# Narrower gram blocks relayed two rows at a time, expert work pulled into the last recurrent step, and constant products on an idle TensorE

## What is computed

```python
def ff_step(W, inp):                                   # fast weights, per head
    v_old = jnp.einsum('bhij,bhj->bhi', W, kt)
    W = W + (bt * (vt - v_old))[..., :, None] * kt[..., None, :]
    z = jnp.einsum('bhij,bhj->bhi', W, qt)
def rec_step(carry, inp):                              # 16 steps, each needs the last one's h
    q_rec = jax.nn.softmax(h, axis=-1)
    v_old = jnp.einsum('bhij,bhj->bhi', R, kt)
    R = R + (bt * (vt - v_old))[..., :, None] * kt[..., None, :]
    h = zt + jnp.einsum('bhij,bhj->bhi', R, q_rec)
...
logits = jnp.mean(x, axis=1) @ Wr + br                 # x: normalised h, 16 x 128 x 64
routing_weights = jax.nn.softmax(logits, axis=-1)
expected_loads = routing_weights.sum(axis=0) * (N / B)
scale = jnp.where(expected_loads > capacity, capacity / expected_loads, 1.0)
routing_weights = jax.nn.softmax(routing_weights * scale, axis=-1)
top_w, top_i = jax.lax.top_k(rw_tok, K); top_w = jax.nn.softmax(top_w, axis=-1)
h = jax.nn.gelu(jnp.einsum('nd,edf->enf', xf, W1) + b1[:, None, :])
y = jnp.einsum('enf,efd->end', h, W2) + b2[:, None, :]  # weighted over the experts, added to x
```

## Times and profile before

| | us |
|---|---|
| three runs | 750.50, 737.28, 741.24; median 741.24 |
| the profiled execution, its own time | 740.56 |
| its span in the trace | 738.7 |
| granted TensorE clock, mean over the span | 0.91 |

### The profile page before, as it was taken

The page is one execution under the profiler, slowest core; times in us unless marked ns, Lnnn a source line. Parts: engine busy times, 40 slices in busy tenths (PEclk is TensorE's granted clock), DMA queues, the critical chain, the costliest instruction groups (busy, mean ns, idle before and its releaser), DMA issues.

```text
span 738.7 us, 12304 instructions
## 1 busy us (share of the span) xinstructions
PE 606.3 (82%) x4657; PEld 477.8 (65%) x4657; DVE 445.8 (60%) x1113; ACT 280.9 (38%) x502; POOL 360.0 (49%) x414
## 2 busy tenths in 40 slices
PE   6889999999987707788877888456999698899996
PEld 3657777785556606677776777352678487785776
DVE  3643444236667756787899999952553736663533
ACT  0075453528966602111110000006553337566550
POOL 1696333218018836797899998143463300001334
PEclk9999999999989956888999999755999869999999
DMA  7000000000004450000000000000000000000000
GB/s 242 1 1 1 2 1 1 0 1 1 0 10 75 78 88 4 1 1 1 1 1 1 1 1 1 0 1 0 1 1 1 1 1 2 1 2 1 8 8 14
DMA packets 10699, 10.35 MB, mean 14 GB/s; under 512 B 5905, under 2 KB 9681, under 8 KB 10385
## 3 DMA queue, kind: packets, MB, share of 16 engines
q1 hardware_dynamic: 7424, 7.12, 3.6%
q0 software_dynamic: 2496, 2.04, 2.0%
q10 hardware_dynamic: 720, 0.41, 0.3%
HBM read 5.70 MB, written 0.52 MB: 8 GB/s over the span
## 4 chain that ended last, share of the span: by engine, by line
PE 55%; DVE 26%; ACT 7%; DMA 4%; issue 4%; POOL 3%; SPq 0%; ACTq 0%; DVEq 0%; POOLq 0%
PE bank L1059 8%; PE bank L1047 7%; DVE features L1743 6%; DVE bank L1777 5%; DVE features L1766 5%; PE bank L1315 4%; PE bank L1136 4%; PE bank L1333 4%; PE bank L1331 4%; PE bank L1403 2%; PE bank L1096 2%; PE bank L1391 2%; PE bank L1127 2%; PE bank L1105 2%; DMA RK<-in_wf 1%
## 5 line engine op out<-in xcount | busy, mean ns | idle before, releaser
L1136 PE MATMUL bank<-ident,features 128*128 128x128 f32 x920 | 126.9, 297 | 63.1 <-DVE features L1743 39.3
L1136 PEld LDWEIGHTS bank<-ident,features 128*128 128x128 f32 x920 | 113.8, 155 | 73.4 <-DVE features L1743 48.0
L506 POOL TENSOR_TENSOR features<-UV,coefs 128x1024 f32<-128x1024 f32 (+1 forms) x64 | 117.6, 1864 | 25.7 <-DVE UV L1730 12.5
L1743 DVE TENSOR_TENSOR features<-UV,bank 128x1024 f32<-128x1024 f32 (+3 forms) x64 | 66.2, 1066 | 0.9
L685 ACT ACTIVATE G<-bank,cols 128x512 f32<-128x512 f32 x64 | 43.3, 687 | 49.5 <-PE bank L1047 49.5
L1047 PE MATMUL bank<-xs,weights 128*128 128x512 f32 x128 | 60.2, 615 | 2.3 <-ACT xs L676 2.3
L1059 PE MATMUL bank<-weights,G 128*128 128x128 f32 x512 | 59.8, 275 | 0.0
L1059 PEld LDWEIGHTS bank<-weights,G 128*128 128x128 f32 x512 | 58.4, 192 | 0.0
L349 POOL TENSOR_SCALAR rstd<-mv 128x4 f32<-128x4 f32 x8 | 1.9, 238 | 112.2 <-DVE mv L361 112.2
L752 ACT ACTIVATE hsT<-bank 128x256 f32<-128x256 f32 x16 | 6.2, 385 | 102.3 <-PE bank L1136 102.3
L1127 PE MATMUL bank<-features 32*128 32x136 f32 x768 | 34.8, 320 | 10.5 <-DVE G L1703 4.1
(11 more groups left out here) (312 smaller groups left out, 1350.6 us busy)
## 6 DMA issues: line engine op xcount, KB each, us to landing
weights<-in_w SPq DMA_DIRECT2D x2, 1024.0 KB, 11.8
features<-in_tok SPq DMA_DIRECT2D x1, 768.0 KB, 6.3
weights<-in_ew SPq DMA_DIRECT2D x4, 128.0 KB, 3.0
weights<-in_ew SPq DMA_DIRECT2D x2, 256.0 KB, 2.9
coefs<-G POOLq DMA_DIRECT2D x20, 25.5 KB, 3.9
coefs<-xs POOLq DMA_DIRECT2D x20, 25.5 KB, 5.2
coefs<-weights POOLq DMA_DIRECT2D x20, 25.5 KB, 5.3
coefs<-sx POOLq DMA_DIRECT2D x18, 25.5 KB, 5.0
```

What stands on the lines that cost most here:

```text
L506: pool.tensor_tensor(out, u, co, ALU.mult).then_inc(s["held_p"], 1)
L1136: last = mm(out[:, P * k:P * k + P], x[:, P * k:P * k + P], ident[:], is_transpose=True, start=first and k == 0, stop=last_ and k == n - 1 ...
L1743: dve.tensor_tensor(out, u, co.unsqueeze(3).broadcast_to([P, R, NH, DH]), ALU.mult)\
```

## The change

Groups of positions become four (GB = 4, NG = 32), and two of them are done together: NR = 16 rounds. A round's products are 48 of 64 x 68, written to the lower and the upper 64 rows of the eight banks. Copies have 204 columns instead of 408. A relay moves 32 rows of 408 to two adjacent partitions, so a round has four relays of 52,224 bytes: two from SP, two from POOL, none from ACT. Six half-size staging buffers lie in G, xs and weights. Sums for steps 4 to 15 move into steps 0 to 4. The statistics and the normalisation of chunk 0 move into steps 5 and 8; its turn, products and GELUs move into step 15, ahead of the rec read-outs. `out_projection` of the last step comes ahead of the means; the three exponentials run without GELUs between them, and chunk 1's GELUs follow. Nine products of `ident` and `rows` follow the grams, one and three more stand around the router's products.

```diff
-GB = 8
+GB = 4
 NG = P // GB
+NR = NG // 2
-NS = 4
+NS = 6
+REWARM = 9
...
-        stage = [b.rearrange("p (b c s) -> p b c s", b=GB, s=SL)
-                 for b in (G[:].rearrange("p g n -> p (g n)")[:, 0:GB * ROWC], XS[:, 0:GB * ROWC], WA[:, 0:GB * ROWC],
-                           SX[:, 0:GB * ROWC])]
+        stage = [b[:, n * GB * ROWC:(n + 1) * GB * ROWC].rearrange("p (b c s) -> p b c s", b=GB, s=SL)
+                 for b in (G[:].rearrange("p g n -> p (g n)"), XS[:], WA[:]) for n in range(2)]
...
         def expert_bank(k, c, e):
+            if k == 0 and c == 0:
+                return bank[4 + e % 2]
...
         def relay(eng, g, j):
-            b = NG * j + g
-            eng.dma_start(CF[b:b + 1, 0:T * ROWC].rearrange("p (t x) -> p t x", t=T),
-                          stage[g % NS][j:P:GB, j].rearrange("p c s -> p (c s)"))\
+            b, x = NG * j + 2 * g, g % NS
+            eng.dma_start(CF[b:b + 2, 0:T * ROWC].rearrange("p (t x) -> p t x", t=T),
+                          stage[x][j:P:GB, j].rearrange("p c s -> p (c s)"))\
...
-                for j in range(0, 3):
+                for j in (0, 1):
                     relay(sp, g, j)
...
-                for j in range(3, 6 if g == NG - 1 else GB):
+                for j in (2, 3):
                     relay(pool, g, j)
...
+                if t == 2 * CH - 1:
+                    rstd_pool(pool, ch, ("f0", 0), CH)
                 held(t)
...
-            for j in (6, 7):
-                relay(act, NG - 1, j)
...
+                if t == T - 1:
+                    experts(0, 0)
+                    expert_gelus(0, 0)
                 state(t)
+            experts(0, 1)
             act.wait_ge(s["mean_mm"], 1)
             act.activation(meanT[:], bank[7][0:D, 0:T], ACT.Copy, scale=1.0 / P).then_inc(s["mean_ready"], 1)
-            experts(0, 0)
             for j in range(3):
                 act.wait_ge(s["r_sub"], j + 1)
                 act.activation(rsel[0:T, j, :], rsel[0:T, j, :], ACT.Exp).then_inc(s["r_exp"], 1)
-                expert_gelus(0, 0, 2 * j, 2 * j + 2)
-            expert_gelus(0, 0, 6, E)
+            expert_gelus(0, 1, 0, 4)
...
                         for j in range(4):
                             x = slice(DH * j, DH * j + DH)
-                            last = mm(bank[4 * k + j][:, GB * SL * n:GB * SL * n + GB * SL],
-                                      feat[left + k][x, g, 0:T].rearrange("p s b -> p (s b)"),
-                                      feat[right + k][x, g].rearrange("p s b -> p (s b)"), start=True, stop=True)
+                            for h in range(2):
+                                last = mm(bank[4 * k + j][D * h:D * h + D, GB * SL * n:GB * SL * n + GB * SL],
+                                          feat[left + k][x, 2 * g + h, 0:T].rearrange("p s b -> p (s b)"),
+                                          feat[right + k][x, 2 * g + h].rearrange("p s b -> p (s b)"), start=True, stop=True)
...
+            def idle_products(b, n):
+                for k in range(n):
+                    mm(b[:, 0:512], ident[:], rows[:, 0:512], start=True, stop=True)
+            pe.wait_ge(s["load_rows"], 48)
+            idle_products(bank[7], REWARM)
...
                 queries(t)
+                if t == T - 1:
+                    pe.wait_ge(s["load_experts"], 16 * 17)
+                    pe.wait_ge(s["pad"], 2)
+                    turn_x(0, 0)
+                    expert_up(0, 0)
                 read_out("rec", t, reads_of("rec", t))
...
+            expert_up(0, 1, 2, 4)
+            pe.wait_ge(s["x_gelu"], E)
+            idle_products(bank[4], 1)
             pe.wait_ge(s["r_prob"], 1)
             mm(bank[7][0:T, 96:96 + E], ones[0:T, 0:T], rout[0:T, 0, :], start=True, stop=True).then_inc(s["load_mm"], 1)
-            expert_up(0, 0, 2, 6)
+            turn_x(0, 2)
+            idle_products(bank[4], 3)
             pe.wait_ge(s["r_spread"], 1)
...
+                if t == CH + 1:
+                    x_stats(0)
+                if t == 2 * CH:
+                    x_apply(0)
+                if t == 0:
+                    normalisers(slice(CH, T))
+                if t == 1:
+                    ch.settle()
+                    strengths(slice(CH, T))
+                if t >= 2 and t + 2 < 2 * CH - 1:
+                    query_scale(t - 1)
                 if t + 1 < T:
                     next_query(t + 1)
```

More of the change, by code:

```diff
@@ L658, in _ @@
         def _(act):
-            ch = Chain(act, s["act_chain"])
             for t, n in ((embT, "embT"), (wupd, "wupd")):
@@ L1786, in read_coefficients, with x_stats @@
                 ch.settle()
+            def x_stats(c):
+                norm_stats(dve, ch, ("f0", c), [H[:, t, :] for t in range(CH * c, CH * c + CH)])
             def x_apply(c):
```

188 lines of the change are left out of this document (94 added, 94 removed).

## The result

The changed kernel takes 766.8 us (median of 4 executions, 765.1 to 772.0) against 739.9 us: a ratio of 1.039, 95% interval 1.033 to 1.045. It is slower by 27 us where 28 us less were forecast. The profiled execution took 765.1 us, with a span of 763.2. From here on every time is the median of those executions of a kernel that lie within 1.5% of its fastest one, which leaves out a few slower ones, such as the 750.5 us of the kernel before.

The account below looks back on a forecast made before the run. Transfers at 70 to 85 GB/s were taken to bound the relays, usually DVE the steps, and a chain of small things the stretch behind. Terms summed to -27.8 from 740.56, giving 712.8 us; own range 706 to 720, 8 in 10 699 to 736.

Parts of the forecast that it names:

- The relays, -8.3: Relay stretch: at 85 GB/s, 3.34 MB take 39.3 us, so the last relay lands at 260.9 instead of 269.18.
- third rival: Relays: writes jam in half as many places, rate halves to 36 to 42 GB/s, 752 to 766 us; chance 0.08.
- The second rival: Relays: few engines serve each two-row transfer, last relay lands at 281.6, +12.4, 733 us; chance 0.18.
- Preparation, -3.0: From last relay to POOL's first product: 3.95 us instead of 7.0, with less scaling ahead of the steps.
- Steps, +4.0: Steps: sums moved into early steps and chunk 0's statistics and normalisation in steps 5 and 8 together add 4.0 us.
- -1.5 for the clock: Start of steps: nine constant products end 2 us ahead of the first step and raise TensorE's clock; bounds -4, +4.
- -0.5 for step 15: Step 15: turn and eight expert products fill an idle hole, state saved at 484.1 instead of 484.6; bounds -1.5, +3.
- To the router's first product, -8.5: From the end of the rec products: reordered projection, statistics and normalisation bring the router's first product at 490.6, 8.5 us less.
- Router, -3.7: Router's first product to weights, 13.4 us before: exponentials no longer wait for GELUs and table changes, 3.7 us less.
- weights to bias, -4.6: From router weights to the bias being added: only the bias work remains, 3.4 us instead of 8.0.
- To the end of the first expert_down, -1.7: From added bias: TensorE stops after two tiles until DVE finishes positional logits; 11.1 us against 12.8.

Follow-up runs that it names:

- the variant without the jam: Changed kernel with the two element groups of a round g and g + 16, so each relay's two destination rows lie 16 apart: 732.5 us, 0.990.

## Why the prediction was wrong

**The relays, -8.3 forecast, +32.1 measured.** The step that failed is the rate: "I take the transfers' own rate, 85 GB/s", because "what set the pace before is still there". It carried the rate of before over to rounds that write to other rows. The text had the right mechanism as its third rival (all bytes of a round to four pairs of neighbouring rows, half as many places, the rate halved to 36 to 42 GB/s, last landing at 300 to 314) and gave it 0.08. The windows read 42 to 45 where all wait (52 at the start), the whole stretch 39, the landing was 301.24, and the variant with rows 16 apart takes the loss back. What was held against that rival, rates over 80 with three neighbouring rounds in flight, was no evidence: in the kernel before, the rows of one round are spread over eight groups of four, and three neighbouring rounds still keep to much the same eight. The second rival (few engines, 0.18) falls as the cause: its transfers are fast once their rows lie apart. Nor would the forecast have held without the jam. No window of the earlier trace rows reads more than 83 GB/s, and 3.34 MB in the 50.6 us of before are 66 on average; the variant without the jam lands its last relay at 268.1, not at 260.9, and takes 732.5 us, which is outside the forecast's own 706 to 720.

**Preparation, -3.0.** Right, 3.1, and the experiment that moved the work back lost 2.2 us in this place.

**Steps, +4.0, -1.5 for the clock, -0.5 for step 15.** Measured +6.9 to the end of the rec products, some 5 us more than the sum. Two terms had the wrong size. The sums in steps 1 to 4, priced at +2.0, cost nothing that shows. The work on chunk 0 was priced at +2.0, with POOL's part in it "hidden; at most +1.3"; it costs 7.7 us. The 0.98 us of a normalisation was carried into step 8, where it takes 5.14 beside POOL's products, and POOL's part was not hidden, since POOL runs ahead and has to wait for DVE there. All variants of the changed kernel, with late and with early relays, take 146.6 to 147.3 us from step 5's addition to step 14's, and the kernel before 139.1 (137.6 with its rounds reordered), so this loss is in the steps themselves; the kernel without sums in the steps has it too (146.8). That it is chunk 0's work is read from the traces: no run moved it back. The clock's -1.5 did not come, because the nine products end 10 us ahead of the landing and the clock falls; where they end in time the traces show 1.4. Of step 15, the end of the rec products is where it was, and the copy of the last state comes 1.79 us behind it instead of 2.75.

**To the router's first product, -8.5.** The order of events was right, but one duration was carried over from before, 0.98 us for the last normalisation, and POOL's products, which the change moves beside it, make it 4.12, the same mistake as in step 8. With those products moved back, the copy of the state stands 7.3 us ahead of the router's first product; with 1.8 us from the end of the rec products to that copy it is 9.1, the figure of the forecast.

**Router, -3.7, and weights to bias, -4.6.** Both right to about 0.1 us; no table load stands between the exponentials.

**To the end of the first expert_down, -1.7.** Here the mechanism was seen, a stop after two tiles until DVE reads the first, but it was sized with DVE's logits at 7.1 us. POOL's scaling of expert weights, which before was over 1 us ahead of those logits, now runs beside them (540.68 to 548.72), and the eight TENSOR_SCALAR take 5.90 us where they took 2.14; the whole block takes 11 us, and TensorE's two later tiles run at a granted clock of 0.50 after their stop, where the two before ran at 1.00 (7.09 us instead of 3.79). That is 7.5 us off. The stretch behind gave 5.0 us back, which wasn't foreseen and is in the main luck: 3.8 us of it fall between two DVE instructions of the later attention (589.24 to 603.41 before, 619.80 to 630.22 after), where TensorE does the same work with a granted clock of 0.50 from 595 to 605 before and of 1.00 from 626 to 631 now.

In sum the relays account for 40 of the 54 us between forecast and result, these terms for 12 (19.5 were forecast besides the relays, 7.6 came), and the rest is that of the medians to the profiled executions.

## What to carry to other kernels

A transfer's destination rows are part of its cost: when an edit changes which partitions are written at the same time, price it by how many different groups of four rows they touch, and not by bytes and the number of transfers alone, and try another assignment of rows before giving up the idea. A duration taken from the profile before holds only with the same neighbours: for each instruction that an edit moves, look at what POOL or DVE then runs beside it, and whether the engine that gets it runs ahead and will now wait there. And when two banks feed a reader, put its reads into a long list of other work, not behind it.

## What the runs showed of the hardware that was not expected

- Writes into neighbouring rows share a way in, and by these distances it is four rows wide: with one-row transfers to pairs 1 or 2 rows apart the relays end at 304, with 4, 8 or 16 at 275 to 278.
- The median relay of POOL's takes 7.2 us from issue to landing with its two rows side by side and 4.0 us with them 16 apart, in transfers otherwise alike.
- Four TENSOR_SCALAR of DVE's take 4.12 instead of 0.98 us beside two TENSOR_TENSOR of POOL's (3.75 us together), and 5.14 beside two others in step 8. By the Trainium skill, SBUF — State Buffer, Who interferes with whom, the two share a port pair that only one holds at a time; these rows agree.
- TensorE's granted clock is 0.50 all through the relay stretch with the halved tiles, in the changed kernel and in the variant with 16 apart that isn't held up by transfers, where it was 1.00 with tiles of full width. What that costs a round wasn't measured.
- TensorE's full clock in the first 20 us of the steps, against 0.50 to 0.78, is worth 1.4 us up to the first addition in the traces, and less than the times of the whole kernel can tell (0.7 us between medians).
